# Moving one layer-norm application from ScalarE to GpSimd, and in the last steps to VectorE

## What is computed

```
x = x + L0_xattn(ctx, layernorm(x))       # 16 heads, queries x, keys and values from ctx
x = x + L0_ffn(layernorm(x))              # 8 experts, mixed by how often each is chosen
x = x + L1_xattn(layernorm(x), ctx, ctx, mask)      # one head of width 256
x = x + L1_ffn(layernorm(x))              # 8 experts, top 2 for each token
layernorm(x) = (x - mean) / sqrt(var + 1e-5)
```

## Time and profile before

| what | value |
|---|---|
| times of three runs | 1298.08, 1302.93, 1303.08 us; median 1302.93 us |
| the profiled execution's own time | 1298.08 us |
| its span, first to last instruction | 1296.3 us |
| mean granted clock of TensorE, of full speed | 0.952 |
| PE busy | 1102.2 us (85%) |
| DVE busy | 883.0 us (68%) |
| POOL busy | 580.7 us (45%) |
| ACT busy | 533.8 us (41%) |
| middle phase | about 641 to 1030 us |

### The profile page before, as it was taken

How to read it: one execution, slowest core, us unless ns; L and a number is a source line. 1 busy time by engine, 2 the same in 40 slices (tenths; PEclk the granted TensorE clock), 3 DMA queues, 4 the chain that set the end, 5 groups by cost and what they waited for, 6 DMA issues and landing times. The chain is left out here.

```text
span 1296.3 us, 33451 instructions
## 1 busy us (share of the span) xinstructions
PE 1102.2 (85%) x9766; PEld 795.7 (61%) x9767; DVE 883.0 (68%) x2673; ACT 533.8 (41%) x1088; POOL 580.7 (45%) x866
## 2 busy tenths in 40 slices
PE   4799998999999999998489997997987289989883
PEld 2477776776767677775336554554555267777772
DVE  4668776786777777775267886886887445555552
ACT  2255554554555555543212322222223145444441
POOL 4544445443544445530014553554556344444554
PEclk9999999999999999997789998998997689999997
DMA  4333333332333233320155443543554145445543
GB/s 128 90 88 80 76 84 84 79 82 65 84 79 88 68 81 83 72 51 2 47 162 144 146 149 113 164 152 105 152 153 149 38 100 84 80 75 85 82 81 37
DMA packets 126269, 121.95 MB, mean 94 GB/s; under 512 B 39266, under 2 KB 116530, under 8 KB 126002
## 3 DMA queue, kind: packets, MB, share of 16 engines
q1 hardware_dynamic: 104434, 92.82, 26.2%
q0 software_dynamic: 21728, 27.93, 11.6%
HBM read 69.36 MB, written 22.43 MB: 71 GB/s over the span
## 5 line engine op out<-in xcount | busy, mean ns | idle before, releaser
L585 DVE TENSOR_REDUCE smax<-psum 112x1 f32<-112x375 f32 x512 | 257.2, 539 | 68.0 <-PE psum L323 54.0
L498 ACT ACTIVATE probsT<-psum 125x896 f32<-125x896 f32 x192 | 172.6, 918 | 83.1 <-PE psum L336 82.4
L1447 POOL DMA_INDIRECT out_dram<-y,token_at x70 | 115.8, 1654 | 128.8 <-DMA out_dram<-y,token_at 101.5
L323 PE MATMUL psum<-k_stack,q_stack 96*112 96x375 f16 x512 | 150.0, 349 | 23.3 <-DVE smax L585 15.3
L323 PEld LDWEIGHTS psum<-k_stack,q_stack 96*112 96x112 f16 x512 | 60.5, 131 | 77.7 <-DVE smax L585 57.1
L1525 ACT ACTIVATE h<-psum,b 128x256 f32<-128x256 f32 x140 | 58.8, 471 | 119.5 <-PE psum L1481 98.3
L988 POOL DMA_INDIRECT dispatch_dram<-rows,slots_at x64 | 63.4, 991 | 96.6 <-DVE slots_at L1291 82.9
L177 POOL DMA_DIRECT2D q_stack<-q_lo x128 | 68.7, 542 | 81.6 <-DVE q_lo L646 55.6
L336 PE MATMUL psum<-q_stack,k_stack 97*125 97x224 f16 x768 | 101.5, 262 | 0.2 <-ACT probsT L498 0.2
L357 PE MATMUL psum<-probsT,v_aug 125*32 125x112 f32 x3072 | 98.2, 272 | 1.2 <-issue 0.9
L1012 PE MATMUL psum<-xT_hi,we_hi 128*128 (+1 forms) x256 | 72.4, 366 | 23.9 <-DVE acc L1180 8.9
(11 more groups left out here) (213 smaller groups left out, 2590.2 us busy)
## 6 DMA issues: line engine op xcount, KB each, us to landing
ctxT<-in_ctxT_dram SPq DMA_DIRECT2D x64, 375.0 KB, 4.0
ctx_rows<-in_ctx_dram SPq DMA_DIRECT2D x32, 375.0 KB
rows_e<-dispatch_dram SPq DMA_DIRECT2D x70, 136.0 KB
w_raw<-in_w_dram SPq DMA_DIRECT2D x32, 256.0 KB
q_stack<-q_hi SPq DMA_DIRECT2D x256, 28.0 KB, 1.9
k_stack<-k_hi SPq DMA_DIRECT2D x128, 46.9 KB, 2.0
k_stack<-k_hi POOLq DMA_DIRECT2D x128, 46.9 KB, 2.3
k_stack<-k_lo SPq DMA_DIRECT2D x128, 46.9 KB, 2.0
```

The source lines that it names most:

```text
L323: nc.tensor.matmul(psum[0:S, 4 + s, 0:KV], q_stack[0:96, b4, h // 2, s * S:(s + 1) * S], k_stack[0:96, b4, h // 2, 0:KV], start=True, stop ...
L498: nc.scalar.activation(probsT[:, p, c, 8 * hg:8 * hg + 8, :].rearrange("p (k h) q -> p k (h q)", k=2), psum[0:KC, 2 * (n % 2):2 * (n % 2) ...
L585: nc.vector.reduce_max(smax[:, (u - LAG_B) % 2, h:h + 1], psum[0:S, 4 + h % 2, 0:KV], AX.X).then_inc(m["max_done"], 1)
L1447: nc.gpsimd.indirect_dma_start(dram["out"], bass.IndirectOffsetOnAxis(token_at[:, p, n:n + 1], 0), y[:, p, n, :], None, compute_op=ALU.add ...
```

## The change

The tile ln_shift, its instruction on POOL, ScalarE's instruction and the semaphore shift3 go. In steps with f on, POOL computes the normalised row itself, as (x3 - mean) x rstd, in the place where ln_shift stood. In the tail steps DVE does the same, behind the second mixture result's place in its list and ahead of first and second; there it waits for ln_rstd.

```
-                    wait(pool, m["x3n_rdy"], cnt(t, ur - 1, 1, 1))
-                    apart(pool)
-                    nc.gpsimd.tensor_scalar(ln_shift[:], ln_mv[:, 1, 0:1], ln_rstd[:, 1, :], -1.0, ALU.mult, ALU.mult).then_inc(m["shift3"], 1)
+                    if f:
+                        wait(pool, m["rs3"], v)
+                        wait(pool, scattered[ur % ROW_SLOTS], sent(t, ur - ROW_SLOTS))
+                        apart(pool)
+                        nc.gpsimd.tensor_scalar(rows[:, ur % ROW_SLOTS, 0:D], x3[:, ur % 2, :], ln_mv[:, 1, 0:1], ln_rstd[:, 1, :], ALU.subtract, ALU.mult).then_inc(m["x3n_rdy"], 1)
...
-                if r:
-                    wait(act, scattered[ur % ROW_SLOTS], sent(t, ur - ROW_SLOTS))
-                    apart(act)
-                    wait(act, m["rows_set"], 1)
-                    apart(act)
-                    wait(act, m["shift3"], cnt(t, ur, 1, 1))
-                    nc.scalar.activation(rows[:, ur % ROW_SLOTS, 0:D], x3[:, ur % 2, :], ACT.Identity, bias=ln_shift[:],
-                                         scale=ln_rstd[:, 1, :]).then_inc(m["x3n_rdy"], 1)
...
+                if r and not f:
+
+                    v = cnt(t, ur, 1, 1)
+                    wait(dve, m["rs3"], v)
+                    wait(dve, m["x3nT_done"], cnt(t, ur - 1, 1, 1))
+                    wait(dve, scattered[ur % ROW_SLOTS], sent(t, ur - ROW_SLOTS))
+                    nc.vector.tensor_scalar(rows[:, ur % ROW_SLOTS, 0:D], x3[:, ur % 2, :], ln_mv[:, 1, 0:1], ln_rstd[:, 1, :], ALU.subtract, ALU.mult).then_inc(m["x3n_rdy"], 1)
```

More of the change, by code:

```diff
@@ L751, in middle_phase @@
     ln_rstd = sb("ln_rstd", [S, 2, 1], F32)
-    ln_shift = sb("ln_shift", [S, 1], F32)
     x2n = sb("x2n", [S, D], F32)
@@ L826, in middle_phase @@
         cum_rdy token_rdy scattered0 scattered1 scattered2 scattered3 x3_out0 x3_out1 pads_out w_in0 w_in1 w_hi_rdy w_lo_rdy rows_set late_in tally_done table
-        eps2 rs2 eps3 rs3 shift3 mask_rdy""".split()
+        eps2 rs2 eps3 rs3 mask_rdy""".split()
     m = {n: sem("m_" + n) for n in names}
@@ L954, in step @@
                     rstd("ag3", "eps3", "rs3", 1, v)
-                    wait(pool, m["rs3"], v)
-                    wait(pool, m["x3n_rdy"], cnt(t, ur - 1, 1, 1))
-                    apart(pool)
-                    nc.gpsimd.tensor_scalar(ln_shift[:], ln_mv[:, 1, 0:1], ln_rstd[:, 1, :], -1.0, ALU.mult, ALU.mult).then_inc(m["shift3"], 1)
+                    if f:
[3 more added lines that the diff above has]
+                        nc.gpsimd.tensor_scalar(rows[:, ur % ROW_SLOTS, 0:D], x3[:, ur % 2, :], ln_mv[:, 1, 0:1], ln_rstd[:, 1, :], ALU.subtract, ALU.mult).then_inc(m["x3n_rdy"], 1)
                 if a:
```

## The result

| | before | after |
|---|---|---|
| median of four runs | 1303.01 us (1298.08 to 1305.44) | 1319.14 us (1309.57 to 1322.15) |
| ratio, 95% interval | | 1.0127 (1.0092 to 1.0162) |
| profiled execution's span | 1296.3 us | 1319.9 us |
| DVE busy | 883.0 us | 918.6 us |
| POOL busy | 580.7 us | 598.8 us |

The direction was the forecast one. The time lies 1 us above the range of 1298 to 1318 and 8 above the forecast of 1311. The changed kernel was timed a second time beside the experiments: ratio 1.0139 (1.0112 to 1.0166).

The account below looks back on a forecast made before the run. The prediction took a VectorE-GpSimd loop of 10.3 us a step as the bound. Loop +11.0 and tail -0.2 made +10.8 us: 1308.9 on the profiled execution, 1313.7 on the median; forecast 1311, range 1298 to 1318.

Parts of the forecast that it names:

- What sets the step: Middle phase: a loop of 6.2 us through VectorE and 4.1 us through GpSimd makes each step 10.3 us.
- the hold moves from unscaled to the instructions ahead of it: Regular steps: the 0.67 us hold on unscaled goes; one of about 1.0 comes on first, second or chosen.
- the faster rival: Regular steps: second slips ahead of w_lo and chosen isn't held; -5.9 us in all, 1292 to 1297, chance 0.16.
- The rival of no change: Regular steps: w_lo stays in place or the holds trade places at the same price; 1298 to 1303, chance 0.17.
- The length of GpSimd's new instruction: GpSimd in 26 steps: the 112x256 normalisation takes 0.50 us, between 0.45 from below and 0.75 from above.
- case (b): Regular steps: w_lo holds second to 3.28, so VectorE's next operation starts at 4.42, +0.47 us a step.
- The rival called longer: Regular steps: GpSimd's new operation takes 0.75 us, w_lo follows without a gap; +0.8 a step, 1313 to 1318, chance 0.12.
- the term of the loop: Steps before the last six: 13 regular, six irregular and the first two with a send together add 11.0 us.
- the three cases: Regular steps: chosen, second or first is held by w_lo, costing +0.27, +0.47 or +0.61 us; 0.45 was taken.
- the first two steps with a send: Start of the sends: ln_rstd comes later, mask_add and w_lo run without a gap; +0.6 us each.
- where max is late: Three irregular steps: gap_exp, w_hi and w_lo shift later, chosen is held to about 3.9; +0.70 us each.
- The tail: Last six steps: +0.2 us in each of four, -0.3 and -0.7 in the last two; sum -0.2 us.

Follow-up runs that it names:

- 1: Kernel before with unscaled moved on VectorE behind the fourth mixture result, after w_lo: regular steps 9.85 us, ratio 0.9952.
- 6: Changed kernel with GpSimd's w_lo computed on 8 of the 512 columns of each piece: regular steps 10.11 us; no ratio given.
- 2: Changed kernel with VectorE doing the normalised row in all 32 steps and GpSimd in none: regular steps 11.2 us, ratio 1.0101.
- 5: Kernel before with the tail half alone: ScalarE normalises in the 26 mixture steps, VectorE in the last six; ratio 0.9994.
- 7: Changed kernel with GpSimd's new instruction as multiply and add with constants 1 and 0, row not normalised: regular steps 10.55 us; no ratio given.
- 10: Changed kernel with eight forms of GpSimd's new instruction, one per step of a turn: 0.40 us for constant multiply with add, 1.1 and 1.25 with a subtract.
- 9: Kernel before with GpSimd normalising in 26 steps, ln_shift and ScalarE in the last six: ratio 1.0135; both kernels reprofiled, the changed one at 1.0139.

## Why the prediction was wrong in size and right in kind

- *What sets the step* (slots_at, the DMAs, ln_rstd, x2n): right. x2n waits for ln_rstd in every kernel here (24 to 27 of 32 times), and a regular step's length follows VectorE's stretch between x2n and slots_at: 6.19 us before, 7.41 after, with 4.1 us from there to x2n in both.
- *VectorE is held while GpSimd works through a wide tile, and the hold moves from unscaled to the instructions ahead of it:* right, and shown by moving either side: unscaled late (1), w_lo narrow (6), mask_add earlier (2, 5). chosen, the kind for which no row of before spoke, is held too (6, 7), and so is gap. This rules out the faster rival. The rival of no change fell too, since w_hi did start earlier (1.21); that w_lo stood at 2.79 in the changed kernel, which was to be a sign of a wrong prediction, came from the length of the row ahead of it. With 0.41 us there w_lo came at 2.12 (7). The rule is coarser than the rows, though: in some places an instruction of the kinds held passes beside GpSimd's new one (below).
- *The length of GpSimd's new instruction:* this step failed. "I take 0.50, since it streams one tensor", with 0.45 and 0.75 as ends; it is 1.25. The line between ln_shift and mask_add mixed forms: ln_shift is multiply and multiply over one column, mask_add multiply and add, the new instruction subtract and multiply, and that pair costs 0.7 us more than multiply and add over 256 columns (10). The upper end was no bound at all: a tensor_tensor of the same shape is another operation, not the dearest form of this one. With 0.41 us in its place the prediction's regular step came out to 0.04 (7). With 1.25, its case (b) comes close to the measured step: with second held to 3.97, chosen starts at 4.00, unscaled at 4.90 and the new x3 at 5.11 instead of 3.95, +1.16. Measured were 5.14, and 11.56 - 10.32 = +1.24 for the step. Which of the three is held, the prediction's working doesn't say for this length. The rival called longer had the right picture, a row without a gap, but with 0.75 us and 1313 to 1318 it stopped short as well.
- *The sum:* +10.8 us against +16.1. In the middle phase the term of the loop, +11.0, was +21.9 in the kernel that has this half alone (347.6 against 325.7). The middle of the three cases, 0.45 a step, was between what 0.41 us gives (0.23) and what 1.25 us gives (1.24), and so hid the error in part. Two more terms were too high and did the same: +0.6 for each of the first two steps with a send was +0.07 and +0.02, and +0.70 where max is late fails at the length that was assumed (-0.3 with 0.41 us, in 7). That the total came within 8 us of the measured one is luck as well: the middle phase lost twice what was forecast, and the whole lost 7 us less than the middle phase, which the prediction had no term for.
- *The tail:* +0.2 a step was +0.5 in three steps against two of the profiles of before, and nothing against the third. I had seen that unscaled might meet w_lo, but not that mask_add would hold gap. The gain behind the last steps, -1.0, isn't shown: from the last x2n to the last phase's first DMA, a stretch that also holds the fourth of these steps, the changed kernel took 1.5 us less than before, but the kernel with the tail half alone took 58.4 us, 0.9 more.
- *The last phase* was taken as untouched. In the profiles it was 5.6 us shorter. There it goes with the tail half (9), in which the mean DMA takes 1.57 to 1.59 us against 1.65 to 1.66, with the same median of 1.55 or 1.56; why 12 of 70 are longer in the one sort is open. In timed runs neither half shows it: the tail half alone gained no 6 us (0.9994, interval 0.9966 to 1.0022), and the loop half alone lost no 6 us more than the whole change (9). So why the whole lost 16.1 us where its middle phase lost 23.1 is open.

The Trainium skill (SBUF — State Buffer, "SBUF: two separate sides") says that VectorE and GpSimd share a port pair that is an exclusive lock for a whole instruction, against VectorE instructions with a two-port mode or two SBUF inputs. The holds of chosen, gap and unscaled, each with two inputs, agree; first and second read one tile, and whether they ran in a two-port mode no row shows. What the rows add is that a held instruction may wait through several GpSimd instructions that follow without a gap (second, 2.06 us, through three). It isn't always so: in 6 second got in between two of them. And some aren't held at all where the rule would have it, as chosen in one step of the changed kernel, 0.17 us in the midst of GpSimd's 1.25:

```profile
721.59 0.17 DVE L1243 TENSOR_TENSOR chosen<-first,second 112x8 f32<-112x8 f32 x1
...
720.69 1.25 POOL L958 TENSOR_SCALAR rows<-we,ln_mv,ln_rstd 112x256 f32<-112x256 f32 x1 [0.31 <-POOL ln_rstd L943]
```

What decides was not found.

## What to carry to other kernels

Before moving work to GpSimd, list which VectorE instructions run beside it, and look for small ones whose duration swings and whose end coincides with a GpSimd instruction: their place in the list is worth more than the work moved, and moving one line gave 0.5% where the change lost 1.3%. Such a hold isn't there each time that the two engines overlap, so look at several steps. A shift of GpSimd's tiles in time, even from relieving a third engine, moves such a hold to another instruction. Price a GpSimd instruction by a row with the same pair of operations, or measure it by itself; a row of the same engine and shape isn't enough.

## What was not expected of the hardware

- GpSimd's tensor_scalar over 112x256 took 0.40 us for multiply and add with constants, 1.1 us as soon as one of the two is a subtract, and 0.89 us for one multiply alone. One multiply costs twice as much as multiply and add together. Two per-partition operands add 0.15.
- A VectorE instruction over eight columns was held 1.8 us beyond its usual 0.22.
- Identical code took 668 to 684 us to the first x2n over the profiles, while the median regular step of the middle phase was equal to 0.03 us in the profiles of one kernel.
- In the last phase, whose code is the same in all kernels, 12 of the 70 indirect DMAs took 2.07 to 2.10 us in some kernels and 1.55 to 1.75 in the others (9).
